# Keys and queries of a multi-mode delta rule: from normalised, turned windows to planes by feature with factors by token, and unread matmuls among the merges

## The chip, the cores and the metric

The kernel runs on one core of a Trainium2 chip. The metric is the device time of one launch in microseconds, the median of several runs. Engines are named as in the profile: PE (TensorE), DVE (VectorE), ACT (ScalarE), POOL (GpSimd) and SP (the queue that issues all transfers here).

## What is computed

The reference is a linear attention with a gated delta rule, followed by a mixture of experts, both with residuals. B=8 batches, T=512 tokens, D=128, H=8 heads, M=8 modes, DK=DV=64. All is 32-bit float.

```python
q, k, v = x@Wq, x@Wk, x@Wv                     # x is layer-normalised; (B,T,H,64)
beta, tg = sigmoid(x@Wbeta), sigmoid(x@Wtg)    # (B,T,H,M)
qr = _l2norm(_rotary(q, cos, sin)) * scale     # by mode: angles differ
kr = _l2norm(_rotary(k, cos, sin))
g = log(clip(tg * rho, 1e-6))
def step(S, inp):                              # over T, for each mode, batch, head
    S = S * exp(g)
    kv = einsum('mbhk,mbhkv->mbhv', k_t, S)
    S = S + k_t * ((v_t - kv) * beta)
    return S, einsum('mbhk,mbhkv->mbhv', q_t, S)
o = einsum('tmbhv,hm->bthv', ys, softmax(mode_logits)) * sigmoid(x@Wg)
x = x + o.reshape(B, T, H*DV) @ Wo             # then x + experts(layernorm(x))
```

A rotation does not change a vector's length, so the norm can be taken of q and k before it.

## The kernel before

`prepare` has two stages, and `recurrence` and `experts` follow, each behind a barrier of all engines (`fresh`).

**Projections** (`project`). A batch is 512 tokens in four tiles of 128. For each tile PE makes q, k, the gates z and v, with tokens as rows of the result (L285 to L294, 512 columns each but z). ACT copies q, k and v out of PSUM and squares q and k; DVE sums the squares by head (L418, L420). A batch later DVE multiplies keys and queries by one over their norm into `win` (L466), and POOL writes the first half of each once more with its sign turned (L504). `win` goes to memory as KQ_s, 192 floats for a token and head. `in_order` interleaves the tiles of batch b with the later work on batch b-1. ACT's chain at a batch's end is: square roots, exponentials, the copy of xT (L324), on which PE's next batch waits.

**Recurrence.** 64 sequences (head, batch), one in each step, `emit`. In step k the engines prepare sequence n+1 and run sequence n at the same time. Modes lie in 4 pairs, two halves of 64 partitions. Preparing: PE turns the window of keys and queries into features as rows (`transposes`, L1011, four groups of 8 matmuls) and ACT copies it to `kqT` (L793), one step ahead of its use; DVE rotates with the tables (`rotate`, L893, L894, L901), PE makes eight blocks of scores (L1053, L1057) and DVE multiplies them by decays (L926); DVE transposes them into lanes and solves 32x32 triangular systems there in 60 short instructions (`eliminate`), and two transposes bring the inverse back, TM (L954) and XO (L955). Running: PE merges the 32-blocks into 64-blocks at the head of the next step (`merge`: m=0 reads TM, L1034; m=1 reads XO and ZM, L1036; each in groups g=0, 1), then eight chunks in series, each through `read_state`, `solve_reads`, `keep_state` (L1108), `write_state`, with ACT moving R, W and S between them.

What sets the order on PE and ACT is a list of jobs (scores, merge(1,1), token_keys, turns) and a table, PE_PLACES and ACT_PLACES, which says how many jobs are taken at each of 16 places among the eight chunks. All matmuls run strictly in that order. One loop turn holds eight steps (one head); a barrier ends it. At k=6 SP also loads the next head's tables `tab`.

**Experts.** For each batch a `head` (gates, output projection, layer norm, routing) is cut into slots between the eight experts. In slots -1 and 0 DVE multiplies o by the gate (L1464), two products of 512 columns in each. PE makes both halves of an expert's hidden units (L1363, L1364) into banks that DVE's product with silu (L1527) must have left.

Of the kernel before, what the change touches and what calls it, by code (L numbers as in the profile page):

```python
# [24 lines left out]
HALF = DK // 2  # L25
# [51 lines left out]
def program(nc, x, Wq, Wk, Wv, Wbeta, Wtg, mode_logits, log_decay, omega_log, Wg, Wo, gate_w, w13, w2,  # L77
# [6 lines left out]
    KQ_s = dram("KQ_s", (H, B, 128, NT, 2 * WIN))  # L84
# [8 lines left out]
    with ExitStack() as whole:  # L93
# [7 lines left out]
        def fresh():  # L101
# [6 lines left out]
                c_mat, c_pos, c_col, ident, XN_s, KQ_s, V_s, G_s, EG_s, COL_s, TAB_s)  # L108
        recurrence(nc, sems, fresh, c_mat, ident, KQ_s, V_s, G_s, EG_s, COL_s, TAB_s, O_s)
        experts(nc, sems, fresh, x, Wg, Wo, gate_w, w13, w2, c_small, ident, XN_s, O_s, out)  # L110


def prepare(nc, sems, fresh, x, Wq, Wk, Wv, Wbeta, Wtg, mode_logits, log_decay, omega_log,
            c_mat, c_pos, c_col, ident, XN_s, KQ_s, V_s, G_s, EG_s, COL_s, TAB_s):
    with ExitStack() as ctx:
# [4 lines left out]
        wq, wk, wv = sb("wq", [128, H * DK]), sb("wk", [128, H * DK]), sb("wv", [128, H * DV])  # L120
        wbt = sb("wbt", [128, 2 * HM])
# [8 lines left out]
        with nc.Block() as block:  # L130
# [16 lines left out]
            def _(act):  # L147
# [4 lines left out]
                act.activation(modes[:, :, :], modes[:, :, :], ACT.Exp).then_inc(exp_out, 1)  # L152

            @block.vector
            def _(dve):
                v = Chain(dve, dve_s)
                dve.wait_ge(loaded, 11 * 16)
# [19 lines left out]
        project(nc, sems, fresh, x, wq, wk, wv, wbt, rho, tri, ones_c, ident, XN_s, raw, KQ_s, V_s, G_s, EG_s)  # L177
# [3 lines left out]
def project(nc, sems, fresh, x, wq, wk, wv, wbt, rho, tri, ones_c, ident, XN_s, raw, KQ_s, V_s, G_s, EG_s):  # L181

    with ExitStack() as ctx:
# [3 lines left out]
        def ps(name, shape):  # L187
# [7 lines left out]
        qk = sb("qk", [128, 2, 2, NT, H * DK])  # L195
        sqq = sb("sqq", [128, 2, 2, H * DK])
        ssq, less = sb("ssq", [128, 2, 2, NT, H]), sb("less", [128, 2, 2, NT, H])
        win = sb("win", [128, NT, H, 2 * WIN])
# [4 lines left out]
        QB, KB = [ps(f"q{i}", [128, 512]) for i in range(2)], [ps(f"k{i}", [128, 512]) for i in range(2)]  # L203
        VB, ZB = ps("v", [128, 512]), ps("z", [128, NT, 2 * HM])
        GB, TB = ps("g", [128, 2, NT, HM]), ps("t", [128, 512])

        (l_x0, l_x1, l_x2, dve_s, xn_done, xt_done, xt_copied, pe_q, pe_k, pe_z, pe_v, freed_q, k_copied, freed_k, freed_v,
         summed, std_in, std_out, ss_in, ss_out, logs_in, logs_out, decay_in, g_done, sums, gt_done, raw_s, exp_in, exp_out,
         lowered, flipped, q_done, halves, put_x0, put_x1, put_v0, put_v1, put_g, put_k) = sems[:39]
        l_x, put_x, put_v = (l_x0, l_x1, l_x2), (put_x0, put_x1), (put_v0, put_v1)  # L210

        def in_order(begin, tile, after, end):
# [1380 lines left out]
```

## Time and profile before

| | us |
|---|---|
| median of 3 runs | 4784.18 (4780.45 to 4792.02) |
| the profiled execution, its own time | 4793.02 |
| its span in the trace | 4790.8 |
| PE busy | 4015.4 (84%) |
| DVE busy | 3652.5 (76%) |
| ACT busy | 2902.2 (61%) |
| POOL busy | 371.3 (8%) |

A busy share says how long an engine had work, not that it set the time. The rows below give starts in microseconds from the span's start; "idle before" is how long the engine had stood before an instruction, with the instruction that released it. The granted clock of PE is given as a share of 2.4 GHz.

### The profile page before, as it was taken

The numbers are of one execution on the slowest core, as the hardware profiler recorded it, in microseconds if no ns is written. First come the engines' busy times: TensorE is split into PE (matmuls) and PEld (weight loads), VectorE is DVE, ScalarE is ACT, GpSimd is POOL, SyncE is SP. The second block draws the span as 40 slices with busy tenths as digits, with TensorE's granted clock in tenths as the row PEclk, the third lists the DMA queues.
The fourth block names the chain that finished last, engine by engine and source line by source line (L and its number), as shares of the span: only waits on it lengthen the run. The fifth ranks groups of instructions, "written<-read, shape, count | busy, mean of one in ns | idle before, by whom it ended". The sixth has DMA issues, their size and how long they took to land. (4 is left out here: it accounts for less than half of the span.)

```text
span 4790.8 us, 195228 instructions
## 1 busy us (share of the span) xinstructions
PE 4015.4 (84%) x85713; PEld 3307.7 (69%) x85713; DVE 3652.5 (76%) x7742; ACT 2902.2 (61%) x9736; POOL 371.3 (8%) x156
## 2 busy tenths in 40 slices
PE   5502999889988998889889988898899889987999
PEld 2201777777777777777777777777777777775666
DVE  6754888778877887788778877887788778854655
ACT  5742666666666666666666666666566666654443
POOL 1221000000000000000000000000000000000000
PEclk8755889889888998899889988998899889988999
DMA  4675222322232223222322231223122312203110
GB/s 119 167 182 133 52 51 56 83 53 52 52 87 53 52 52 87 53 52 52 87 53 52 52 87 47 57 52 87 40 59 58 82 44 58 57 10 83 36 31 7
DMA packets 283082, 314.77 MB, mean 66 GB/s; under 512 B 135768, under 2 KB 182752, under 8 KB 278112
## 3 DMA queue, kind: packets, MB, share of 16 engines
q1 hardware_dynamic: 282208, 301.99, 26.7%
q8 instruction: 687, 11.26, 1.0%
q14 instruction: 187, 1.53, 0.1%
HBM read 232.70 MB, written 69.21 MB: 63 GB/s over the span
## 5 line engine op out<-in xcount | busy, mean ns | idle before, releaser
L926 DVE TENSOR_TENSOR run_SC<-run_SP,run_DB 128x512 f32<-128x512 f32 x512 | 350.1, 687 | 474.6 <-PE run_SP L1057 468.3
L943 DVE TENSOR_TENSOR run_XL<-run_XL,run_EL 128x30 f32<-128x30 f32 (+14 forms) x1920 | 637.3, 332 | 66.0
L942 DVE TENSOR_TENSOR run_EL<-run_AL,run_XL 128x30 f32<-128x30 f32 (+14 forms) x1920 | 636.7, 332 | 66.0
L1053 PE MATMUL run_SP<-run_KP 64*32 64x128 f32 x8192 | 624.8, 302 | 24.5 <-DVE run_KP L901 12.7
L980 POOL TENSOR_TENSOR run_DB<-run_DB,run_below 128x2048 f32<-128x2048 f32 x64 | 297.9, 4655 | 3613.7 <-DVE run_XL L943 3487.9
L801 ACT ACTIVATE run_DB<-run_DB,run_col 128x64 f32<-128x64 f32 x2048 | 537.3, 337 | 12.0 <-POOL run_DB L980 4.2
L1053 PEld LDWEIGHTS run_SP<-run_KP 64*32 64x32 f32 x8192 | 465.6, 119 | 101.8 <-issue 50.0
L859 ACT COPY run_S<-run_KS 128x256 f32<-128x256 f32 x448 | 166.9, 373 | 556.5 <-PE run_KS L1118 556.5
L808 ACT ACTIVATE run_KD<-run_PR,run_col 128x64 f32<-128x64 f32 x2048 | 471.6, 327 | 12.9 <-PE run_PR L1073 6.8
L846 ACT ACTIVATE run_R<-run_KS,run_col 128x64 f32<-128x64 f32 x1792 | 416.0, 323 | 102.8 <-PE run_KS L1082 102.4
L1057 PE MATMUL run_SP<-run_KP 64*32 64x64 f32 x8192 | 454.5, 243 | 0.0
L1036 PE MATMUL run_PR<-run_XO,run_ZM 32*64 32x32 f32 x8192 | 422.9, 275 | 36.9 <-ACT run_ZM L778 36.6
L893 DVE TENSOR_TENSOR run_tmpv<-run_tab,run_kqT 128x512 f32<-128x512 f32 x512 | 372.2, 727 | 104.7 <-ACT run_kqT L793 37.6
L1011 PE MATMUL run_PR<-ident,run_win 128*64 128x128 f32 x4096 | 299.8, 283 | 178.0 <-DMA run_win<-KQ_s 154.0
L1036 PEld LDWEIGHTS run_PR<-run_XO,run_ZM 32*64 32x64 f32 x8192 | 406.1, 202 | 50.6 <-ACT run_ZM L778 41.5
L850 ACT ACTIVATE run_Sdec<-run_S,run_decay 128x64 f32<-128x64 f32 x1536 | 413.5, 364 | 0.0
L1094 PE MATMUL run_WP<-run_V,run_XN 64*64 64x64 f32 x8192 | 375.9, 237 | 39.9 <-issue 39.1
L1011 PEld LDWEIGHTS run_PR<-ident,run_win 128*64 128x64 f32 x4096 | 238.9, 141 | 208.7 <-DMA run_win<-KQ_s 154.3
L1073 PE MATMUL run_PR<-ident,run_KP 64*64 64x64 f32 x8192 | 294.1, 221 | 92.8 <-ACT run_KD L808 90.8
L1094 PEld LDWEIGHTS run_WP<-run_V,run_XN 64*64 64x64 f32 x8192 | 325.0, 152 | 65.9 <-issue 65.9
L1073 PEld LDWEIGHTS run_PR<-ident,run_KP 64*64 64x64 f32 x8192 | 260.8, 134 | 146.5 <-issue 142.2
L1125 PE MATMUL run_OB<-run_W,run_SC 128*64 128x64 f32 x4096 | 361.5, 234 | 0.5 <-ACT run_W L853 0.5
(201 smaller groups left out, 7588.8 us busy)
## 6 DMA issues: line engine op xcount, KB each, us to landing
run_DB<-G_s SPq DMA_DIRECT2D x256, 256.0 KB
run_EG<-EG_s SPq DMA_DIRECT2D x128, 512.0 KB, 8.9
run_tab<-TAB_s SPq DMA_DIRECT2D x128, 256.0 KB, 10.5
KQ_s<-proj_win SPq DMA_DIRECT2D x32, 768.0 KB, 7.8
run_win<-KQ_s SPq DMA_DIRECT2D x64, 384.0 KB, 3.1
TAB_s<-tab_tab SPq DMA_DIRECT2D x128, 128.0 KB, 2.4
run_V<-V_s SPq DMA_DIRECT2D x128, 128.0 KB, 2.6
V_s<-proj_vv SPq DMA_DIRECT2D x64, 128.0 KB, 3.1
```

Source lines behind the costliest of these rows:

```text
L801: last = act.activation(DB[:, p, c, :], DB[:, p, c, :], ACT.Exp, bias=col[:, par, 0, p, c:c + 1])
L808: last = act.activation(KD[:, par, p, c, :], token_rows[:, c % 2, p, :], ACT.Copy, scale=col[:, par, 2, p, c:c + 1])
L846: last = act.activation(R[:, p, :], KS[:, 0, p, :], ACT.Copy, scale=col[:, now, 1, p, c:c + 1])
L850: last = act.activation(Sdec[:, p, :], S[:, c % 2, p, :], ACT.Copy, scale=decay[:, now, p, c:c + 1])
L942: v.link(dve.tensor_tensor(e, bcast(AL[:, r + 1:, r], 2, done), bcast(XL[:, r, 0:done], 1, rows), ALU.mult))
L943: less = dve.tensor_tensor(XL[:, r + 1:, 0:done], XL[:, r + 1:, 0:done], e, ALU.subtract)
L1011: last = pe.matmul(PR[1][64 * e:64 * e + 64, 128 * i:128 * i + 128], win[:, i, off:off + DK], ident[:, :], start=True, stop=True)
L1036: last = pe.matmul(to[64 * e:64 * e + SPAN], ZM[two, p, c, :], XO[two, p, c, :], start=True, stop=True)
L1053: pe.matmul(out[64 * e:64 * e + C, p].rearrange("p (z u) i -> p z (u i)", z=2), KP[f, par, p, t0:t1], KP[f, kq, p, t0:t0 + SPAN], start=Tr ...
L1057: last = pe.matmul(out[64 * e + C:64 * e + SPAN, p, 0::3, :], KP[f, par, p, t1:t1 + C], KP[f, kq, p, t1:t1 + C], start=True, stop=True)
L1073: last = pe.matmul(token_rows[f, z, p, :], KP[f, par, p, t0:t0 + SPAN], ident[f, f], start=True, stop=True)
L1094: last = pe.matmul(WP[f, 0, p, :], XN[f, p, c, :], V[f, now, c, :], start=(p == 0), stop=(c == 0 and p == PAIRS - 1))
```

## The change

Keys and queries are no longer normalised and no longer turned. `project` computes them with features as rows: the weights are now the stationary operand and xT the moving one. A plane of the negated first halves comes from a third matmul with negated weights `wn`. The sums of squares are matmuls of the squares with `pair`, two columns of ones. Norms become factors by token: beta is divided by the squared key norm (added to the argument of its logarithm), v is multiplied by the key norm when DVE takes it out of PSUM, and one over the query norm goes to memory as RQ_s and is applied to o in `experts`. KQ_s has planes of 512 tokens for each feature, which six transfers put straight into `kqT` (`load_kq`). POOL has no work left in `project`.

In the recurrence the turns on PE and their copies on ACT are gone, the places are shifted accordingly, `token_keys` alternates between two banks, and `stay_busy`, a matmul whose result nothing reads, stands twice ahead of merge(0,0) (not in the first step of a loop turn), once behind it and once behind merge(0,1).

```diff
-    KQ_s = dram("KQ_s", (H, B, 128, NT, 2 * WIN))
+    KQ_s = dram("KQ_s", (H, B, 2, DK + HALF, T))
+    RQ_s = dram("RQ_s", (B, 128, NT, H))
...
+                for query, w in enumerate((wk, wq)):
+                    act.activation(wn[:, query], w[:, :].rearrange("p (h d) -> p h d", h=H)[:, :, 0:HALF], ACT.Copy, scale=-1.0).then_inc(exp_out, 1)
...
+                def square_sums(b, i):
...
+                    for query in range(2):
+                        pe.wait_ge(freed[query], n + 1)
+                        for t in range(NT):
+                            last = pe.matmul(SB[:, query, t, 2 * i:2 * i + 2], squares[:, n % 2, query, 128 * t:128 * t + 128], pair[:, :],
+                                             start=True, stop=True)
+                    last.then_inc(pe_ss, 1)
...
-                    pe.matmul(QB[n % 2][:, :], lhsT, wq[:, :], start=True, stop=True).then_inc(pe_q, 1)
-                    pe.matmul(KB[n % 2][:, :], lhsT, wk[:, :], start=True, stop=True).then_inc(pe_k, 1)
+                    for query, w in enumerate((wk, wq)):
+                        if n:
+                            pe.wait_ge(freed[query], n)
+                        pe.matmul(FB[query][:, :], w[:, 128 * i:128 * i + 128], xT[:, b % 2], start=True, stop=True).then_inc(pe_f[query], 1)
+                    if n:
+                        pe.wait_ge(freed_n, n)
+                    pe.matmul(NB[:, :], wn[:, i % 2, 4 * (i // 2):4 * (i // 2) + 4, :].rearrange("p h d -> p (h d)"), xT[:, b % 2],
+                              start=True, stop=True).then_inc(pe_n, 1)
...
+                def values(b, i):
+                    dve.wait_ge(pe_v, NT * b + i + 1)
+                    dve.tensor_tensor(vv[:, b % 2, i, :, :], VB[:, :, :], bcast(root[:, b % 2, 0, i, :], 2, DV), ALU.mult).then_inc(valued, 1)
...
-            @block.gpsimd
-            def _(pool):
-                def after(b, i):
...
+                    def load_kq(n):
+                        of = KQ_s.rearrange("h b z f t -> (h b) z f t")[bass.ds(n, 1)]
+                        for e in range(2):
+                            at = 64 * e
+                            for rows, planes, feats in ((slice(at, at + DK), 0, slice(0, DK)), (slice(at, at + HALF), 1, slice(HALF, DK)),
+                                                        (slice(at + HALF, at + DK), 1, slice(DK, DK + HALF))):
+                                sp.dma_start(kqT[rows, planes::2, :], of[:, :, feats].rearrange("a z f t -> f (a z) t")).then_inc(l_kq, 16)
...
                         if more:
                             n = n0 + (k + 2)
-                            sp.wait_ge(scored, SUPER * k + 2)
-                            if k + sets:
-                                sp.wait_ge(pe_t, 4 * (k + sets))
-                            load_win(n)
+                            sp.wait_ge(rot_k, NT * (k + 1))
+                            sp.wait_ge(rot_q, NT * (k + 1))
+                            load_kq(n)
                             sp.wait_ge(scored, SUPER * (k + 1))
                             load_g(n)
...
-                            turn = [(lambda r=r: transposed(k + sets, r)) if more else (lambda: None) for r in range(4)]
-                            jobs += ex + keys[0:4] + turn[0:2] + keys[4:6] + turn[2:3] + keys[6:8] + turn[3:4]
+                            jobs += ex + keys
...
-                                if k + sets:
-                                    dve.wait_ge(act_t, 4 * (k + sets))
+                                here(dve, l_kq, 6, k)
...
+                        def stay_busy():
+                            pe.matmul(KS[:, 0].rearrange("p a v -> p (a v)"), ident[:, :], Sdec[:, :, :].rearrange("p a v -> p (a v)"),
+                                      start=True, stop=True)
...
                         if runs:
+                            if k:
+                                stay_busy()
+                                stay_busy()
                             merge(0, 0)
+                            stay_busy()
                             merge(0, 1)
+                            stay_busy()
                             merge(1, 0)
...
+                            dve.wait_ge(l_r[b % 2], 16 * (b // 2 + 1))
+                            heads = o[:, b % 2, i, :].rearrange("p (h v) -> p h v", h=H)
+                            dve.tensor_tensor(heads, heads, bcast(rq[:, b % 2, i, :], 2, DV), ALU.mult).then_inc(scaled, 1)
+                            dve.wait_ge(scaled, NT * b + i + 1)
                             dve.tensor_tensor(o[:, b % 2, i, :], o[:, b % 2, i, :], gate[:, i, :], ALU.mult).then_inc(gated, 1)
```

The order of PE at the end of a step and the head of the next, before (from the second to the third step of a loop turn; OB are the outputs, PR the bank of merges and turns):

```order
L1011 MATMUL run_PR<-ident,run_win 64x128 x8
L1103 MATMUL run_WP<-run_R,run_XN 64x64 x8
L1073 MATMUL run_PR<-ident,run_KP 64x64 x16
L1125 MATMUL run_OB<-run_W,run_SC 64x64 x4
L1011 MATMUL run_PR<-ident,run_win 64x128 x8
L1034 MATMUL run_PR<-run_TM,run_SC 32x32 x64
L1036 MATMUL run_PR<-run_XO,run_ZM 64x32 x32
```

And the same place now:

```order
L1071 MATMUL run_WP<-run_R,run_XN 64x64 x8
L1098 MATMUL run_OB<-run_W,run_SC 64x64 x4
L1081 MATMUL run_KS<-run_Sdec,ident 128x256 x2
L1002 MATMUL run_PR<-run_TM,run_SC 32x32 x32
L1081 MATMUL run_KS<-run_Sdec,ident 128x256
L1002 MATMUL run_PR<-run_TM,run_SC 32x32 x32
L1081 MATMUL run_KS<-run_Sdec,ident 128x256
L1004 MATMUL run_PR<-run_XO,run_ZM 64x32 x32
```

Turns and the last token_keys have left the end of the step; three places of unread matmuls stand around the two first merges.

The order of PE in the projections, one tile of a batch in the steady part, before:

```order
L285 MATMUL proj_bank_q<-set_wq,proj_xT 128x512
L288 MATMUL proj_bank_k<-set_wk,proj_xT 128x512
L291 MATMUL proj_bank_z<-set_wbt,proj_xT 128x128
L294 MATMUL proj_bank_v<-set_wv,proj_xT 128x512
```

And now:

```order
L313 MATMUL proj_bank_f<-proj_xT,set_wk 128x512
L313 MATMUL proj_bank_f<-proj_xT,set_wq 128x512
L316 MATMUL proj_bank_n<-proj_xT,set_wn 128x512
L320 MATMUL proj_bank_z<-set_wbt,proj_xT 128x128
L301 MATMUL proj_bank_s<-set_pair,proj_squares 128x2 x8
L331 MATMUL proj_bank_v<-set_wv,proj_xT 128x512
```

A fourth matmul of 512 columns and eight of 2 columns have come into each tile.

## Rows read from the trace of the kernel before

**Rows 1.** Busy time by stage: us, then PE, PEld, DVE, ACT, POOL busy (x), PEclk, DMA share, GB/s
```profile
0.00:277.00 277.00, 135.22 (x384) 68.44 (x384) 170.00 (x311) 161.94 (x285) 50.21 (x69) 0.78 0.56 152
...
476.00:4250.00 3774.00, 3367.41 (x81532) 2883.08 (x81534) 3082.93 (x6381) 2425.20 (x8891) 285.69 (x63) 0.88 0.26 59
...
4314.00:4791.00 477.00, 432.80 (x2137) 288.47 (x2137) 268.40 (x831) 201.03 (x284) 0.00 (x0) 0.96 0.18 40
```

**Rows 2.** DVE transpose that ends a step: duration, first and last start
```profile
L955 DVE STREAM_TRANSPOSE run_XO<-run_XL x64: 1881/1936/1999, 476.3 to 4269.4; 128x1024 f32<-128x1024 f32 x64
```

**Rows 3.** DVE waits of the whole recurrence: us, times, longest us
```profile
DVE run_SC L926 <- PE run_SP L1057: 468.3, 300, 5.7
DVE run_tmpv L893 <- ACT run_kqT L793: 37.6, 7, 6.2
DVE run_tmpv L893 <- issue: 37.3, 6, 7.0
```

**Rows 4.** DVE timeline, two steps: start, us, instruction, [idle before <-releaser]
```profile
1991.12 1.94 DVE L955 STREAM_TRANSPOSE run_XO<-run_XL 128x1024 f32<-128x1024 f32 x1
...
2006.67 0.69 DVE L926 TENSOR_TENSOR run_SC<-run_SP,run_DB 128x512 f32<-128x512 f32 x1 [1.51 <-PE run_SP L1057]
...
2011.32 0.69 DVE L926 TENSOR_TENSOR run_SC<-run_SP,run_DB 128x512 f32<-128x512 f32 x1 [0.34 <-PE run_SP L1057]
...
2013.55 0.69 DVE L926 TENSOR_TENSOR run_SC<-run_SP,run_DB 128x512 f32<-128x512 f32 x1 [0.84 <-PE run_SP L1057]
...
2016.92 0.69 DVE L926 TENSOR_TENSOR run_SC<-run_SP,run_DB 128x512 f32<-128x512 f32 x1 [2.08 <-PE run_SP L1057]
...
2020.03 0.69 DVE L926 TENSOR_TENSOR run_SC<-run_SP,run_DB 128x512 f32<-128x512 f32 x1 [0.62 <-PE run_SP L1057]
2023.41 0.69 DVE L926 TENSOR_TENSOR run_SC<-run_SP,run_DB 128x512 f32<-128x512 f32 x1 [2.68 <-PE run_SP L1057]
...
2050.96 1.94 DVE L955 STREAM_TRANSPOSE run_XO<-run_XL 128x1024 f32<-128x1024 f32 x1
...
2073.16 0.69 DVE L926 TENSOR_TENSOR run_SC<-run_SP,run_DB 128x512 f32<-128x512 f32 x1 [1.47 <-PE run_SP L1057]
...
2076.27 0.69 DVE L926 TENSOR_TENSOR run_SC<-run_SP,run_DB 128x512 f32<-128x512 f32 x1 [0.62 <-PE run_SP L1057]
2079.64 0.69 DVE L926 TENSOR_TENSOR run_SC<-run_SP,run_DB 128x512 f32<-128x512 f32 x1 [2.68 <-PE run_SP L1057]
```

**Rows 5.** Two step starts by windows, columns as in rows 1
```profile
1993.00:2010.00 17.00, 16.21 (x304) 14.69 (x301) 15.46 (x26) 9.74 (x27) 0.78 (x1) 0.50 0.09 25
...
2054.00:2061.00 7.00, 6.48 (x114) 5.79 (x114) 7.00 (x13) 5.67 (x16) 0.00 (x0) 0.52 0.01 3
```

**Rows 6.** PE timeline of the later step, columns as in rows 4
```profile
2054.52 3.63 PE L1036 MATMUL run_PR<-run_XO,run_ZM 32*64 32x32 f32 x64 [1.20 <-ACT run_ZM L778]
...
2060.97 2.10 PE L1036 MATMUL run_PR<-run_XO,run_ZM 32*64 32x32 f32 x64
...
2068.01 0.70 PE L1108 MATMUL run_KS<-run_Sdec,ident 128*128 128x256 f32 x2
```

**Rows 7.** The last four us before a rotation that waited for kqT
```profile
2342.00:2346.00 4.00, 2.63 (x56) 2.35 (x56) 0.00 (x0) 2.54 (x12) 0.00 (x0) 1.00 0.09 23
```

**Rows 8.** PE timeline of the projections; all copies of xT, first and last start
```profile
131.74 2.07 PE L285 MATMUL proj_bank_q<-set_wq,proj_xT 128*128 128x512 f32 x2 [11.84 <-ACT proj_xT L324]
...
L324 ACT COPY proj_xT<-proj_bank_t x8: 567/567/586, 26.3 to 215.0; 128x512 f32<-128x512 f32 x8
```

**Rows 9.** PE timeline of the experts: small matmuls, then w13 matmuls
```profile
4471.54 0.96 PE L1341 MATMUL moe_ebank<-moe_gwT,moe_x2T 128*128 128x8 f32 x8
...
4492.40 1.02 PE L1363 MATMUL moe_ebank<-moe_x2T,moe_w13T 128*128 128x512 f32 x2
4493.26 1.02 PE L1364 MATMUL moe_ebank<-moe_x2T,moe_w13T 128*128 128x512 f32 x2
```

**Rows 10.** DVE timeline of the experts: hidden units after the gate
```profile
4490.56 1.28 DVE L1527 TENSOR_TENSOR moe_hid<-moe_sil,moe_ebank 128x512 f32<-128x512 f32 x2
```

More of the change, by code:

```diff
@@ L156, in _ @@
                 v = Chain(dve, dve_s)
+                v.link(dve.memset(pair[:, :], 0.0))
+                for h2 in range(2):
+                    v(dve.memset(pair[64 * h2:64 * h2 + 64, h2:h2 + 1], 1.0))
                 dve.wait_ge(loaded, 11 * 16)
@@ L296, in after, with end @@
+                def end(b):
+                    square_sums(b, NT - 1)
                 def after(b, i):
+                    if b or i:
+                        pe.wait_ge(valued, NT * b + i)
+                    pe.matmul(VB[:, :, :].rearrange("p h d -> p (h d)"), xT[:, b % 2, 128 * i:128 * i + 128], wv[:, :], start=True, stop=True).then_inc(pe_v, 1)
                     if i != 2:
@@ L309, in after @@
                     last.then_inc(sums, 1)
-                in_order(begin, tile, after, lambda b: None)
+                in_order(begin, quarter, after, end)
             @block.scalar
@@ L484, in after @@
                             dve.wait_ge(lowered, B)
[L486 to L508 removed]
+                in_order(begin, quarter, after, end)
         fresh()
@@ L807, in token_keys @@
                             for p in range(PAIRS):
-                                last = act.activation(KD[:, par, p, c, :], token_rows[:, c % 2, p, :], ACT.Copy,
+                                last = act.activation(KD[:, par, p, c, :], token_rows[c // 2 % 2][:, c % 2, p, :], ACT.Copy,
                                                       scale=col[:, par, 2, p, c:c + 1])
                             last.then_inc(kd_done, 1)
-                        if first and k == 0:
-                            for r in range(4):
-                                transposed(0, r)
                         if runs:
@@ L1149, in _ @@
                             kd = [lambda c=c: token_keys(c) for c in range(GROUP)]
-                            wins += more
-                            turned += more
-                            turn = [(lambda r=r: transposes(k + sets, r)) if more else (lambda: None) for r in range(4)]
-                            jobs = sc[0:1] + jobs + sc[1:] + kd[0:2] + turn[0:2] + kd[2:3] + turn[2:3] + kd[3:4] + turn[3:4]
+                            jobs = sc[0:1] + jobs + sc[1:] + kd
                         if not runs:
```

248 lines of the change are left out of this document (94 added, 154 removed).

## The prediction

> **What bounds the kernel now.** I read the stages first [rows 1]: the recurrence, from 476 to 4250 us, is 79% of the span. In it PE is busy 3367 of 3774 us and VectorE (DVE) 3083, so busy shares alone do not name the bound. The order of waiting does. One step (prepare sequence n+1, run sequence n) ends with the DVE transpose run_XO; between its first and its last start lie 63 steps in 3793.1 us, 60.2 us each [rows 2]. DVE's waits in the whole recurrence [rows 3] are 468.3 us for scores from PE (L926), 37.6 us for the turned keys kqT at 7 steps, and 37.3 us of "issue" at 6 of the loop's barriers. Per step that is 7.4 + 0.6 + 0.6 us, which leaves 51.5 us in which DVE works without pause: rotations, scores, elimination, transposes. DVE is therefore the ring that closes each step, and only its waits can be had.
>
> Two steps in a row show what the score waits are made of [rows 4]. From 1991.12 to 2050.96 (59.84 us) they are 1.51 + 0.34 + 0.84 + 2.08 + 0.62 + 2.68 = 8.07 us; in the next step 1.47 + 0.62 + 2.68 = 4.77. The last two, for scores 6 and 7, are the same to 0.01 us in both: they come from PE's place in the order late in the score phase and not from how the step began. What differs is the beginning. The granted clock stood at 0.50, which is 1.2 GHz, for 17 us after the first XO and for nearly 7 us after the second [rows 5]. A merge of 64 rows with ZM as one operand (L1036) takes 3.6 us then and 2.1 us at 2.4 GHz [rows 6]. PE was busy for 16.2 of the 17 us. What preceded both falls was a gap on PE and then the merges, which use 32-row tiles.
>
> **Part 1, the turning goes.** Out of each step go 4 groups of 8 matmuls (16 rows of L1011) and 4 copies to kqT on ScalarE (ACT). In ordinary steps they lie under DVE's elimination, and I take 0 for them. At the seventh step of each group of eight they are late: DVE waits 37.6 us / 7 = 5.4 us for kqT [rows 3], at a time when the DMA share has already fallen to 0.09 [rows 7], so the tables have landed and only the tail of PE and ACT is awaited. Without turns the rotation needs the outputs of PE and the tables. I leave 1 us: 7 x 4.4 = -31 us. Bounds: 0 (the tail is not shorter) and -38.
>
> **Part 2, kqT comes by DMA.** load_kq issues 6 transfers (128 x 4 x 512 floats, 1.05 MB) once all rotations are done, before load_g; in place of one of 128 x 4 x 192 floats, 0.39 MB, near the same point. SP's queue behind them holds load_g and load_eg, which wait for later signals in any case. Nothing needs kqT until the next step, some 35 us later. Price 0; if it starved PE, see rival D.
>
> **Part 3, the unread matmuls.** Each is 2 rows of 128x256, the form of keep_state, 0.63 us at 2.4 GHz by the 2 rows of 0.70 us with their overlap [rows 6]. The one before merge(1,0) and the one between the first merges fall into PE's 1.20 us wait for ZM [rows 6]: 2 x 0.63 = 1.26, so 0.1 us net. The two at the head of a step have no wait ahead of them and run in the gap after the last outputs. At 1.2 GHz they would cost twice that and 1.3 us would lie in the open. What they can give is the clock at 2.4 GHz through merges and first scores. Then the 1.5 us wait and the three others of a slow start go, and 0.62 + 2.68 = 3.3 us per step stays. Between 3.3 and today's mean of 7.4 I take 3.7, near the first, because the fall of the clock has followed the 32-row merges in both rows and full-array matmuls now stand among them; and 3 us more at 14 steps that begin after a barrier or after a table load. 63 x 3.7 + 14 x 3 = 275 us against 468.3: -193 us. Bounds: nothing regained, and 63 x 3.3 = 208, -260 us.
>
> The Trainium skill (TensorE: Matmul & The Clock Gate, HAM oscillation) says that a wait between groups of matmuls is enough to send the clock down again, each time. By it this change could lose: the tail is shorter, so the gap ahead of the first merge grows. That is rival A below. The rows of the two falls agree in that a gap came before both.
>
> **Part 4, the projections.** Per batch PE gets 16 matmuls of 512 columns for 12, and 8 groups of 4 matmuls with 2 moving columns, the sums of squares. A 512-column matmul is 0.86 us at 2.4 GHz (its 2 rows cover 1.02, and 0.86 lie between starts [rows 9]), so +3.4 us. The nearest row for the sums is L1341: 4 matmuls with 8 columns cover 0.96 us, less the same 0.15 of overlap 0.81 [rows 9]: 8 x 0.81 = 6.5 us. Today a batch takes 27.0 us (xT's first and last copy, 7 batches apart), and PE waits 11.84 us of one for xT [rows 8]. Adding 9.9 to the other 15.2 gives 25.1, and of the wait I take 4 us as not to be filled, since square roots, exponentials, two table loads and the copy of xT follow each other there on ACT. 29.1 against 27.0: +2.1 us x 8 = +17, and 1 for the tail. PE becomes the bound of this stage, ACT loses 4 copies and DVE 8 sums and 8 products, which I price at 0. Bounds: 0 (the gap takes it all) and +45, if half of the sums run at 1.2 GHz.
>
> The Trainium skill (TensorE: Matmul & The Clock Gate, Part 1) has starts of small matmuls no closer than about 25 ns; 64 rows at that floor would be 1.6 us a batch, and by it the stage would cost nothing more. The row says 101 ns, and I go by the row.
>
> **Part 5, small terms.** wn and its two ACT copies: +1. First step of all: DVE waits there for tables behind 0.66 MB more, at 152 GB/s [rows 1] +4. Experts: DVE scales o by rq, 32 products of 0.69 us, the form of L926, and 0.04 for each link. Four of them come before the hidden units of 4490.56 [rows 10], whose first half ends at 4491.2; PE's L1363 follows at 4492.40 [rows 9]. 4 x 0.73 = 2.9 us against 1.2 of slack: 1.7 us x 7 batches = +12. Bounds 0 and 20.
>
> **The sum** against the profiled execution: -31 - 193 + 18 + 1 + 4 + 12 = -189 us. That execution took 4793.0 us (span 4790.8), 8.8 above the median of 4784.2; so 4604 in its terms and **4595** in the median's. If everything open came out well (-38 - 260 + 5) it would be 4491; if only half of the clock's part came, 4691.
>
> **Rivals.**
> A, slower: the gap decides. With the turns gone PE ends earlier, the clock is down at the first merge of every step, and the four matmuls run at 1.2 GHz. All steps become like the first of [rows 4], 8.1 us of score waits, plus 1.3 us for the matmuls: 63 x (8.1 + 1.3) = 592 against 468, +124; with -31 and +35 that is +128, 4912. It takes the forecast's gain away from 3.0 us per step on (189 / 63). For it: PE's gaps precede the falls. Against it: full-array rows run at both sides of the gap. 0.06.
> B, no effect on the clock: waits stay at 7.4, hidden at 2.4 GHz: -31 + 35 = +4, 4788. 0.05.
> C, half held: -97 in place of -193, 4691. 0.09.
> D, the transfer: PE's stream is starved of instructions while 1 MB of kq moves in the score phase. Against it: the smaller load near this point leaves no stall in either step of [rows 4]. At the length of the third-last wait, 1.5 us, in each step: +94, 4689. 0.07.
> My forecast: 0.73, with its own range 4520 to 4650.
>
> **Chances and range.** The median moves by under 0.3% (14 us) without meaning, so that is my bound. Faster: forecast, C, D, 0.89, less 0.01 for mishaps with them: 0.88. Same: B, 0.05. Slower: A and what I did not see, 0.07. The range takes C and D in and A and B out: 4520 to 4715.
>
> **What would show it.** The clock over 476 to the end of the recurrence near 0.95 for 0.88. DVE's score waits near 275 us, with waits of 0.6 and 2.7 us still in each step and the 1.5 gone; no kqT row; steps near 55.2 us. PE without its 11.8 us wait in the projections and batches of 29 us. A wait of L1363 for hidden units of some 1.7 us more once a batch in the experts. The prediction is wrong if the clock is at 0.50 at most step starts, or if scores 6 and 7 wait longer than 3.3 us together because DVE, sooner there, meets the same PE.

## The result, and the profile after

The change made the kernel slower: 4917.3 us median (4910.8 to 4926.5) against 4782.3 (4780.5 to 4792.0), a ratio of 1.028, with a 95% interval of 1.026 to 1.030. The forecast was 4595, with a range of 4520 to 4715. The result is that of rival A, which was priced at 4912 and given a chance of 0.06.

The stages of the changed kernel by windows (columns as in [rows 1]), then the transpose that ends a step:

```profile
0.00:277.00 277.00, 215.04 (x942) 134.98 (x942) 116.06 (x240) 143.55 (x246) 0.20 (x4) 0.90 0.54 134
...
514.00:4365.00 3851.00, 3360.27 (x78344) 2802.30 (x78344) 3106.97 (x6427) 2294.21 (x8694) 285.01 (x63) 0.86 0.30 69
```

```profile
L945 DVE STREAM_TRANSPOSE run_XO<-run_XL x64: 1896/1932/1992, 513.9 to 4365.3; 128x1024 f32<-128x1024 f32 x64
```

Against [rows 2] this splits the difference of the two profiled executions (spans 4909.0 and 4790.8, 118 us) into three parts. Up to the first XO: 476.3 became 513.9, +37.6. The 63 steps between: 3793.1 became 3851.4, +58.3. After the last XO: 521.4 became 543.7, +22.3. The forecast had +23, -224 and +12 there, so it failed in the recurrence. The two ends together cost 59.9 us where 35 were priced.

Within the recurrence, 44 of the 58.3 us lie in the 48 steps that are neither the first nor the last of a loop turn (59.37 us for 58.46 in the mean). The eight first ones lost 28 (70.17 for 66.66), and the seven last ones gave 14 back (62.87 for 64.81).

DVE's waits in the changed recurrence, against [rows 3]:

```profile
DVE run_SC L916 <- PE run_SP L1025: 563.8, 301, 5.8
...
DVE run_tmpv L883 <- issue: 31.0, 6, 5.6
```

The row for kqT is gone, as forecast (-37.6). The score waits rose by 95.5 us where they were to fall by 193. The granted clock of the stage is 0.86, lower than the 0.88 of before. One step, among the slowest, shows how. These are PE's rows from the end of one step into the next (start, us, instruction, [idle before <-releaser]); the step's XO starts at 812.14:

```profile
807.03 0.68 PE L1098 MATMUL run_OB<-run_W,run_SC 128*64 128x64 f32 x8 [0.47 <-ACT run_W L844]
807.63 1.13 PE L1081 MATMUL run_KS<-run_Sdec,ident 128*128 128x256 f32 x4
812.30 1.92 PE L1002 MATMUL run_PR<-run_TM,run_SC 32*32 32x32 f32 x64 [3.54 <-DVE run_TM L944]
814.15 1.22 PE L1081 MATMUL run_KS<-run_Sdec,ident 128*128 128x256 f32 x2
815.30 1.92 PE L1002 MATMUL run_PR<-run_TM,run_SC 32*32 32x32 f32 x64
817.15 1.22 PE L1081 MATMUL run_KS<-run_Sdec,ident 128*128 128x256 f32 x2
818.30 3.62 PE L1004 MATMUL run_PR<-run_XO,run_ZM 32*64 32x32 f32 x64
821.85 0.42 PE L1021 MATMUL run_SP<-run_KP 64*32 64x128 f32 x2
```

The same place before the change, XO at 2050.96:

```profile
2048.38 1.04 PE L1011 MATMUL run_PR<-ident,run_win 128*64 128x128 f32 x14
2051.11 2.21 PE L1034 MATMUL run_PR<-run_TM,run_SC 32*32 32x32 f32 x128 [1.69 <-DVE run_TM L954]
...
2058.08 0.42 PE L1053 MATMUL run_SP<-run_KP 64*32 64x128 f32 x2
```

And the granted clock around that step of the changed kernel, by windows:

```profile
807.50:810.50 3.00, 1.27 (x8) 0.74 (x6) 2.66 (x11) 1.38 (x7) 0.25 (x1) 1.00 0.19 43
810.50:831.00 20.50, 18.70 (x356) 16.00 (x358) 16.36 (x23) 7.69 (x19) 4.30 (x1) 0.50 0.07 18
831.00:870.00 39.00, 34.70 (x882) 28.62 (x878) 31.17 (x74) 26.57 (x110) 0.00 (x0) 1.00 0.35 84
```

Before, the turns filled PE's tail and the wait for TM was 1.69 us. Now PE has only the outputs and the two leading unread matmuls there, then stands 3.54 us, and the clock is already at 1.2 GHz when the first merge starts. Both unread matmuls between the merges then take 1.22 us each (0.70 at 2.4 GHz, [rows 6]) in the path to the first scores. The first scores start 9.7 us after XO (821.85 - 812.14), where they started after 7.1 (2058.08 - 2050.96). DVE's waits in this step are on its own timeline:

```profile
830.30 0.69 DVE L916 TENSOR_TENSOR run_SC<-run_SP,run_DB 128x512 f32<-128x512 f32 x1 [4.11 <-PE run_SP L1025]
...
836.32 0.69 DVE L916 TENSOR_TENSOR run_SC<-run_SP,run_DB 128x512 f32<-128x512 f32 x1 [0.42 <-PE run_SP L1025]
...
839.70 0.69 DVE L916 TENSOR_TENSOR run_SC<-run_SP,run_DB 128x512 f32<-128x512 f32 x1 [2.09 <-PE run_SP L1025]
...
842.80 0.69 DVE L916 TENSOR_TENSOR run_SC<-run_SP,run_DB 128x512 f32<-128x512 f32 x1 [0.62 <-PE run_SP L1025]
```

With the last of 2.7 they are 9.9 us; before, the two steps of [rows 4] had 8.07 and 4.77.

Not every step is like this one. In 20 of the 48 ordinary steps the clock is at 1.2 GHz when the first merge starts: these take 60.9 us in the mean, with PE idle for 3.4 us ahead of the merge and the first scores 9.7 us after XO. In 23 it falls later, up to 2.8 us after XO: 58.6 us, 2.6 idle, scores after 8.6. The other five take 56.9. In the kernel before, none of the 48 had the clock down at the first merge, PE stood idle for 1.6 us in the mean (2.7 in the change), and the first scores came after 7.1. So what the ordinary steps lost lies in the 20. (These means are worked out from the trace, as in the table below.)

### The profile page after: what moved, and what is told of

Same layout as the page of the kernel before. It is cut to its first block and busy times, and to the rows that moved or that the text cites. A ratio compares the mean times of both kernels' runs of the same rounds, so it can differ in the third digit from the quotient of the medians.

```text
span 4909.0 us, 189436 instructions
## 1 busy us (share of the span) xinstructions
PE 4081.3 (83%) x82673; PEld 3281.1 (67%) x82673; DVE 3632.5 (74%) x7714; ACT 2740.6 (56%) x9450; POOL 321.1 (7%) x92
## 5 line engine op out<-in xcount | busy, mean ns | idle before, releaser
L916 DVE TENSOR_TENSOR run_SC<-run_SP,run_DB 128x512 f32<-128x512 f32 x512 | 352.2, 688 | 570.5 <-PE run_SP L1025 563.8
L1002 PE MATMUL run_PR<-run_TM,run_SC 32*32 32x32 f32 x8192 | 217.5, 222 | 261.4 <-DVE run_TM L944 132.5
L1004 PEld LDWEIGHTS run_PR<-run_XO,run_ZM 32*64 32x64 f32 x8192 | 393.2, 197 | 47.2 <-ACT run_ZM L782 24.1
L1002 PEld LDWEIGHTS run_PR<-run_TM,run_SC 32*32 32x32 f32 x8192 | 200.7, 137 | 320.4 <-issue 160.5
L1004 PE MATMUL run_PR<-run_XO,run_ZM 32*64 32x32 f32 x8192 | 409.8, 270 | 0.4 <-issue 0.4
L1071 PE MATMUL run_WP<-run_R,run_XN 64*64 64x64 f32 x7168 | 311.1, 227 | 118.2 <-ACT run_R L837 117.3
L1071 PEld LDWEIGHTS run_WP<-run_R,run_XN 64*64 64x64 f32 x7168 | 249.0, 136 | 191.6 <-ACT run_R L837 153.4
```

What stands on the lines that cost most here:

```text
L1002: last = pe.matmul(to[two], SC[one, 0, p, c, C:], TM[one, p, c, :], start=True, stop=True)
L1004: last = pe.matmul(to[64 * e:64 * e + SPAN], ZM[two, p, c, :], XO[two, p, c, :], start=True, stop=True)
L1071: last = pe.matmul(WP[f, 0, p, :], XN[f, p, c, :], R[f, p, :], start=False, stop=(p == PAIRS - 1))
```

## The experiments

Twelve kernels were run. Eleven differ in where unread matmuls (`stay_busy`) stand at the head of a step. `stay_busy` stands at up to six places: ahead of merge(0,0); between the groups of stage one (m=0); behind stage one; in the middle of merge(1,0); behind merge(1,0); in the middle of merge(1,1). The numbers in the table are how many stand at each. "Ordinary" is the mean step among the 48 that are neither first nor last of a loop turn. "Held" is how many of all 63 steps passed without the granted clock leaving 1.00. "Recurrence" is from the first XO to the last. These three are worked out from the starts of XO and the granted clock in each trace. The leading ones are left out in the first step of a loop turn everywhere; in the change, e2, e3 and e10 the two among the merges stand there too. Ratios are against the kernel before on the same chip.

| kernel | base | unread | median us | ratio (95%) | recurrence | ordinary | held |
|---|---|---|---|---|---|---|---|
| before | | none | 4782.3 | 1 | 3793.1 | 58.46 | 0 |
| the change | | 2,1,1,0,0,0 | 4917.3 | 1.028 (1.026 to 1.030) | 3851.4 | 59.37 | 1 |
| e1_no_unread | change | none | 4840.1 | 1.011 (1.008 to 1.015) | 3783.8 | 58.49 | 0 |
| e10_fill5 | change | 5,1,1,0,0,0 | 4909.7 | 1.028 (1.024 to 1.031) | 3843.2 | 59.42 | 5 |
| e3_fill9 | change | 9,1,1,0,0,0 | 4725.7 | 0.989 (0.986 to 0.992) | 3670.8 | 55.97 | 22 |
| e4_fill9_only | change | 9,0,0,0,0,0 | 4796.3 | 1.004 (1.003 to 1.006) | 3735.3 | 57.76 | 0 |
| e9_fill_hold1 | change | 9,1,0,1,0,0 | 4814.4 | 1.008 (1.004 to 1.011) | 3753.5 | 57.72 | 8 |
| e5_fill_hold | change | 9,1,1,1,1,1 | 4734.9 | 0.990 (0.985 to 0.994) | 3675.9 | 56.22 | 38 |
| e2_before_unread | before | 2,1,1,0,0,0 | 4707.2 | 0.982 (0.977 to 0.987) | 3706.9 | 56.74 | 24 |
| e8_before_hold1 | before | 3,1,0,1,0,0 | 4736.0 | 0.991 (0.988 to 0.994) | 3721.1 | 57.56 | 10 |
| e7_before_hold | before | 3,1,1,1,1,1 | 4680.7 | 0.978 (0.974 to 0.982) | 3676.7 | 56.09 | 41 |
| e12_before_six | before | 3,1,1,1,1,0 | 4622.5 | 0.966 (0.964 to 0.968) | 3626.1 | 55.26 | 40 |
| e11_small_tiles | before | 3,1,1,1,1,1 on 32x32 | 4937.2 | 1.033 (1.031 to 1.035) | 3926.1 | 60.74 | 0 |

**e1_no_unread.** All four taken out:

```diff
                         if runs:
-                            if k:
-                                stay_busy()
-                                stay_busy()
                             merge(0, 0)
-                            stay_busy()
                             merge(0, 1)
-                            stay_busy()
                             merge(1, 0)
```

> The changed kernel without its four unread matmuls. Theory G (the gap on PE between the last outputs and the first merge, 3.6 us where it was 1.5, lets the clock fall, and the unread matmuls among the merges, 1.2 us each at 1.2 GHz, then lie in the path): most steps still begin at 1.2 GHz, but the merges reach their second stage about 2 us sooner; 63 x 2 = 126 us less than the changed kernel, 4790 us, about the kernel before. Rival S (the unread matmuls do hold part of the clock, and without them it is worse): over 4920 us. Rival D (the keys' and queries' transfers starve PE): no change, 4917 us.

Measured 4840 us. The direction is theory G's, the size is not: 68 us came back in the recurrence, 1.1 per step for the 2 expected. So the four matmuls lost some 68 us net where they stand. The clock was down at the first merge in 45 of 48 ordinary steps here and in 20 with them, so they do hold something, and cost more than it is worth. The other 60 us of the loss are outside the recurrence.

**e2_before_unread.** The kernel before with the same four (and a memset of Sdec ahead of the loops):

```diff
                         if runs:
+                            if k:
+                                stay_busy()
+                                stay_busy()
                             merge(0, 0)
+                            stay_busy()
                             merge(0, 1)
+                            stay_busy()
                             merge(1, 0)
```

> The kernel before with the four unread matmuls alone added at the changed kernel's places. There the gap at a step's end is 1.5 us, and the two leading ones take 1.1 us of it. Theory G: the gap nearly closes, the clock stays at 2.4 GHz through the merges in most steps, and the waits of a slow start go; 60.2 us per step becomes 56 to 57, some 4570 us. Rival M (the 32-row merges bring the clock down whatever surrounds them, and the unread matmuls only cost): 4800 to 4900 us. In between, 4700 us, if the clock is held in half of the steps.

Measured 4707, the middle case (one of its four executions took 4661). The same four matmuls that cost 68 us in the changed kernel gain 86 in the recurrence of the kernel before. The clock was down at XO's start in no ordinary step, and 24 of 63 steps passed without a fall. The two kernels differ in all the rest of the change; what of it PE's rows show at this place is the end of the step, where the turns and the last token_keys still stand here (mean idle time ahead of the first merge 0.5 us, for 2.7).

**e3_fill9, e4_fill9_only, e10_fill5.** The changed kernel with the gap filled:

```diff
                             if k:
-                                stay_busy()
-                                stay_busy()
+                                for _ in range(9):
+                                    stay_busy()
                             merge(0, 0)
```

e4 also leaves out the one between the groups and the one behind them; e10 has five in place of nine.

> The changed kernel with nine leading unread matmuls in place of two, 0.56 us each at 2.4 GHz, so that PE has work from its last outputs to the first merge (3.6 us gap closed, 0.5 us over). Theory G: the clock stays at 2.4 GHz at most step starts outside barriers, steps take 54 to 55.5 us (the one step of the changed kernel whose clock never fell took 54.03), 48 x 5.5 = 264 us or more less: 4600 to 4650 us, granted clock of the recurrence over 0.93. Rival M (the merges bring it down themselves): 4917 us or more. Rival D: 4917 us or more.

> The same nine leading unread matmuls, and none between the merges. Theory G with the gap at the step's end alone as cause: as with the two between them or a little better, 4580 to 4640 us. If PE's short wait between the merges (1.2 us for ZM) is a second cause of the fall: the clock falls at 2 to 3 us into the step as in the kernel before, and it comes out near 4700 us.

> The changed kernel with five leading unread matmuls, the dose between two (4917 us) and nine (4726 us): 0.56 us each at 2.4 GHz, so the gap ahead of the first merge is 3.6 - 3 x 0.56 = 1.9 us. Theory G (the length of the gap decides): fewer steps begin at 1.2 GHz than with two, time between the two others, 4800 to 4850 us; if any gap under some 2 us is harmless, 4730 us. Rival (it is the number of full-array matmuls that counts and not the gap they close): also in between, but with the clock down at the first merge in as many steps as with two.

With nine, the changed kernel falls from 4917 to 4726, 1.1% under the kernel before. It also rules out rival D: its 22 steps without a fall take 54.1 us (median), 2.7 of them waits, with every kq transfer in place. It misses the 4600 to 4650 that G expected, and its rows show why. PE at the start of a step whose XO is at 2668.9:

```profile
2664.33 4.15 PE L1081 MATMUL run_KS<-run_Sdec,ident 128*128 128x256 f32 x18
2669.04 1.20 PE L1002 MATMUL run_PR<-run_TM,run_SC 32*32 32x32 f32 x64 [0.55 <-DVE run_TM L944]
2670.17 0.70 PE L1081 MATMUL run_KS<-run_Sdec,ident 128*128 128x256 f32 x2
2670.80 1.20 PE L1002 MATMUL run_PR<-run_TM,run_SC 32*32 32x32 f32 x64
2671.93 0.70 PE L1081 MATMUL run_KS<-run_Sdec,ident 128*128 128x256 f32 x2
2672.56 2.05 PE L1004 MATMUL run_PR<-run_XO,run_ZM 32*64 32x32 f32 x64
```

and the clock over it:

```profile
2668.90:2674.60 5.70, 5.56 (x196) 4.72 (x196) 5.67 (x8) 3.67 (x7) 2.62 (x1) 1.00 0.07 23
2674.60:2684.80 10.20, 9.63 (x170) 8.56 (x170) 9.48 (x16) 4.07 (x15) 0.00 (x0) 0.50 0.01 3
```

PE was busy for 5.56 of 5.70 us, and the clock fell all the same, behind the merges. In another step of this run, with XO at 1624.6, PE did not pause at all before the fall:

```profile
1621.60:1630.05 8.45, 8.45 (x206) 7.04 (x204) 8.24 (x12) 3.84 (x7) 4.57 (x1) 1.00 0.22 56
1630.20:1640.20 10.00, 9.74 (x172) 8.54 (x172) 9.28 (x16) 4.01 (x14) 0.00 (x0) 0.50 0.01 2
```

So the gap is not the only cause: falls also come at the end of the 32-row merges, with PE at work throughout. That it is the merges was still an argument here; e5 and e7 put it to the test. e4 and e10 say the same from two sides. Without the two among the first merges the fall comes in every step (none held); with the gap half closed the clock was up at XO's start in all 48 ordinary steps and down at the first merge in 5, but down 4 us after XO in 31, and nothing was gained. Theory G as I had put it, that the gap decides, fell here.

**e5_fill_hold and e7_before_hold.** Three more in stage two, and none in the first step of a loop turn:

```diff
+                                if m == 1 and k and p == 1:
+                                    stay_busy()
                             last.then_inc(pe_m, 1)
+                            if m == 1 and k and g == 0:
+                                stay_busy()
...
+                            if k:
+                                for _ in range(3):
+                                    stay_busy()
                             merge(0, 0)
+                            if k:
+                                stay_busy()
                             merge(0, 1)
+                            if k:
+                                stay_busy()
                             merge(1, 0)
```

(this is the kernel before; the changed one has nine ahead.)

> Nine leading unread matmuls as in the run before, one more in the middle of merge(1,0), one behind it and one in the middle of merge(1,1), in all steps but the first of a loop turn, where now none stands. Theory M2 (what is left of the falls, 5 to 6 us into half of the steps, comes from the 32-row merges of the second stage, which PE works at without a pause): the clock stays at 2.4 GHz through ordinary steps, which take 54 to 55 us for a mean of 56.0, and the first steps of a turn lose two unread matmuls of 1.2 us: 48 x 1.5 + 8 x 2.4 = 91 us less than with nine alone, 4635 us. Rival W (the falls follow short waits of PE in the first scores, so the added matmuls only cost their 0.6 us): 4710 to 4740 us.

> The kernel before, with its turning, norms and projections as they were, and unread matmuls alone: three ahead of merge(0,0) in place of two, one between the merges of the first stage, and one in the middle of merge(1,0), behind it and in the middle of merge(1,1), none in the first step of a loop turn. Theory M2: ordinary steps 54 to 55 us for the 56.7 of the run with four: 4707 - 48 x 2 - 10 = 4600 us. Rival W: 4700 to 4730 us. Against the fill in the changed kernel it shows what the rest of the change is worth once the clock is held: if turning costs nothing under DVE's elimination, this one is faster by the projections and experts, some 50 us less what the late kqT costs at 7 steps (30 us).

M2 was right on the cause: the falls 5 to 6 us into ordinary steps are gone (one is left, in e7), the clock stood at 2.4 GHz through 38 and 41 of 63 steps, and most of the others are the last two or the first of a loop turn. It was wrong on the time: 4735 and 4681. The first of these is what rival W had forecast (4710 to 4740), though its cause is not the one seen. The held steps have 4.6 and 4.2 us of waits (medians) where e3's have 2.7: two of the three new matmuls stand ahead of the first scores, which now come 7.6 and 7.5 us after XO for 6.5, and the third ahead of the second ones. The pair also prices the rest of the change at a held clock, if the nine leading matmuls of the one and the three of the other fill their gaps alike: recurrences of 3675.9 and 3676.7 us, so no gain from taking the turns out shows there. Of the 51 us between the two profiled executions, 40 lie up to the first XO and 13 behind the last.

**e8_before_hold1 and e9_fill_hold1.** Against e7 and e5, none behind stage one, and one in place of three in stage two:

```diff
-                                if m == 1 and k and p == 1:
+                                if m == 1 and k and g == 0 and p == 1:
                                     stay_busy()
-                            if m == 1 and k and g == 0:
-                                stay_busy()
...
                             merge(0, 1)
-                            if k:
-                                stay_busy()
                             merge(1, 0)
```

> The kernel before with three leading unread matmuls, one between the two groups of merge(0,.), and one in the middle of merge(1,0); none in the first step of a loop turn. In the run with seven the clock never fell in ordinary steps, but each step kept 0.8 to 2 us of score waits ahead of the last two, and 0.6 of the seventh. If one unread matmul in the second stage is enough to hold the clock, and the two taken away are 1.2 us of the path: ordinary steps near 54.5 us for 56.1, 4681 - 48 x 1.5 = 4610 us. If the clock falls again at 5 us into half of the steps: 4690 to 4700 us.

> The changed kernel with nine leading unread matmuls, one between the groups of the first stage, and one in the middle of merge(1,0); none in the first step of a loop turn. As for the kernel before: if the clock is held, 4735 - 48 x 1.5 = 4660 us; if it falls at 5 us in half of the steps, 4730 to 4750. Against the run beside it this one should be slower by the projections and the experts, 35 to 60 us, if turning on PE costs nothing once the clock is held.

Both lost: only 10 and 8 steps held, 4736 and 4814 us, each above the bad case of its expectation (4700 and 4750). In 33 and 39 of the 48 ordinary steps the clock fell within 8 us after XO. The two lie 78 us apart for the 35 to 60 expected; 32 of it are in the recurrence.

**e12_before_six.** This is e7 without the unread matmul in the middle of merge(1,1). (e7 has eight unread matmuls and this one seven; the expectations say seven and six.)

```diff
-                                if m == 1 and k and p == 1:
+                                if m == 1 and k and g == 0 and p == 1:
                                     stay_busy()
```

> The best run so far without the unread matmul in the middle of merge(1,1): six for seven. If the clock is held all the same, the first score wait of 0.8 us in ordinary steps becomes 0.2 or none: 4681 - 48 x 0.6 = 4652 us. If it falls at 6 us into a third of the steps: 16 x 2.5 = 40 us more, 4700 us.

Measured 4622.5 us, 3.4% under the kernel before and 6.0% under the change: the fastest here. PE from the end of a step on:

```profile
1976.67 1.56 PE L1118 MATMUL run_KS<-run_Sdec,ident 128*128 128x256 f32 x6
1978.23 1.20 PE L1035 MATMUL run_PR<-run_TM,run_SC 32*32 32x32 f32 x64
1979.36 0.70 PE L1118 MATMUL run_KS<-run_Sdec,ident 128*128 128x256 f32 x2
1979.98 1.20 PE L1035 MATMUL run_PR<-run_TM,run_SC 32*32 32x32 f32 x64
1981.12 0.70 PE L1118 MATMUL run_KS<-run_Sdec,ident 128*128 128x256 f32 x2
1981.74 1.12 PE L1037 MATMUL run_PR<-run_XO,run_ZM 32*64 32x32 f32 x32
1982.80 0.70 PE L1118 MATMUL run_KS<-run_Sdec,ident 128*128 128x256 f32 x2
1983.42 1.12 PE L1037 MATMUL run_PR<-run_XO,run_ZM 32*64 32x32 f32 x32
```

The window over five ordinary steps, and DVE's waits of the recurrence:

```profile
1923.20:2197.60 274.40, 259.50 (x6565) 215.81 (x6566) 246.04 (x512) 190.99 (x706) 22.89 (x6) 1.00 0.25 56
```

```profile
DVE run_SC L927 <- PE run_SP L1062: 308.1, 183, 5.8
DVE run_tmpv L894 <- ACT run_kqT L794: 40.6, 8, 6.8
```

Steps of 54.9 us (274.4 / 5), the clock at 1.00, score waits of 308 us for 468. That is what the forecast had hoped for from the change (275 us, 55.2 us a step), with the turns still in. The held steps have 3.4 us of waits (median) for e7's 4.2.

**e11_small_tiles.** e7 with each unread matmul on a 32x32 tile:

```diff
-                            pe.matmul(KS[:, 0].rearrange("p a v -> p (a v)"), ident[:, :], Sdec[:, :, :].rearrange("p a v -> p (a v)"),
+                            pe.matmul(KS[0:32, 0].rearrange("p a v -> p (a v)"), ident[0:32, 0:32], Sdec[0:32, :, :].rearrange("p a v -> p (a v)"),
                                       start=True, stop=True)
```

> The kernel before with the seven unread matmuls of the best run so far (three leading, one between the groups of stage one and one behind, three in stage two), each on a 32x32 tile of the array and 256 columns in place of 128x128 and 256, so that PE is as long at work on them but with a sixteenth of the array. If what holds the clock is that PE has no pause, it is held as with the large ones: 4680 us, clock near 0.93. If it is how much of the array is at work: the clock falls at 1.7 to 5 us into most steps as in the kernel before, and the matmuls then cost 1.2 us each: 4860 to 4950 us, clock under 0.87.

Measured 4937 us. PE at a step's start, XO at 2092.0:

```profile
2090.82 1.48 PE L1118 MATMUL run_KS<-run_Sdec,ident 32*32 32x256 f32 x6
...
2093.13 0.40 PE L1118 MATMUL run_KS<-run_Sdec,ident 32*32 32x256 f32 x1
2093.16 0.38 PE L1035 MATMUL run_PR<-run_TM,run_SC 32*32 32x32 f32 x14
...
2095.55 1.27 PE L1037 MATMUL run_PR<-run_XO,run_ZM 32*64 32x32 f32 x32 [0.73 <-ACT run_ZM L779]
```

and the clock from 4.5 us behind XO on:

```profile
2096.50:2113.50 17.00, 17.00 (x251) 13.05 (x250) 12.83 (x22) 7.26 (x26) 0.00 (x0) 0.50 0.08 25
```

The three leading ones take 1.48 us, as the large ones do (1.56), and no step was held, against 41 with the large ones. Full-array matmuls hold the clock, these do not. The run is not quite the test it was meant to be: among the merges the small ones run beside them (2093.13 and 2093.16), so that a pause of 0.73 us ahead of stage two stays. That a fall needs no pause is shown by e3's step at 1624.6. A comparison with small matmuls that leave no pause was not run.

**e6_terms_out.** The changed kernel with two computations left out, for the terms outside the recurrence:

```diff
-                        for t in range(NT):
+                        for t in range(1):
                             last = pe.matmul(SB[:, query, t, 2 * i:2 * i + 2], squares[:, n % 2, query, 128 * t:128 * t + 128], pair[:, :],
...
-                    dve.tensor_scalar(ssq[:, b % 2], SB[:, :, :, :], 1e-6, None, ALU.add).then_inc(ss_in, 1)
+                    dve.tensor_scalar(ssq[:, b % 2], bcast(SB[:, :, 0, :], 2, NT), 1e-6, None, ALU.add).then_inc(ss_in, 1)
...
-                            dve.tensor_tensor(heads, heads, bcast(rq[:, b % 2, i, :], 2, DV), ALU.mult).then_inc(scaled, 1)
-                            dve.wait_ge(scaled, NT * b + i + 1)
```

> The changed kernel with two computations left out: three quarters of the square sums on PE in the projections (norms are taken of one tile in four), and the scaling of the attention output by one over the query norm in the experts. If the square sums on PE set the batch (31.0 us for 27.0 before), the last batch's copy of xT comes at some 216 us for 243.8, and the stage of the tables starts 28 us sooner; if the wait for ACT's chain or the transfers of the planes set it, it stays within 5 us. If DVE's scaling is what the experts lost, their 22 us come back. Both: 4867 us; neither: 4917 us.

Measured 4893 us. The copies of xT, here and in the change:

```profile
L358 ACT COPY proj_xT<-proj_bank_t x8: 567/567/587, 26.3 to 226.6; 128x512 f32<-128x512 f32 x8
```

```profile
L358 ACT COPY proj_xT<-proj_bank_t x8: 567/567/585, 26.5 to 243.8; 128x512 f32<-128x512 f32 x8
```

A batch took 27.0 us before [rows 8], 31.0 in the change and 28.6 here. Three quarters of the square sums are worth 17 us of the stage (243.8 to 226.6), not the 28 expected. From the last XO to the end it is 523.5 us for 543.7, so the scaling of o is nearly all of the 22 us that the experts lost. The recurrence, whose code is untouched, took 3877.9 us for 3851.4. Recurrences of one trace each can thus differ by 26 us without a cause in the code, and smaller differences in the table's column prove nothing.

## Why the prediction was wrong

**The frame was right.** DVE's waits set the step, and at a held clock 3.3 us of them stay: 32 of e12's 48 ordinary steps have score waits of 3.3 to 3.5 us, and five steps in a row took 54.9 us each. (Of the 51.5 us that the prediction calls work without pause, 48.9 are DVE's busy time, 3083 / 63; the rest are smaller waits.)

**Part 3 failed, in its last inference.** It said that the clock would hold "because the fall of the clock has followed the 32-row merges in both rows and full-array matmuls now stand among them". The runs show two things that bring the fall, a gap (two leading matmuls against nine) and a run of 32-row merges (e3 against e5), and the four matmuls answer neither in full. I counted the two leading ones as work in the gap and did not subtract what the removed turns had done there: the wait for TM went from 1.69 to 3.54 us in the steps shown. Part 1 had priced the same removal at a gain. The estimate of -193 became +95.5 in score waits. The matmuls were also priced at 0.1 us net among the merges, at 2.4 GHz; at 1.2 GHz they are 1.22 each, and the net cost of all four was some 68 us (e1).

**Rival A** had the direction and nearly the sum: 9.4 us per step of waits and matmuls against a measured 563.8 / 63 = 8.9, and 4912 us against 4917. Partly this is luck. It had +93 us in the recurrence (124 - 31) for the measured 58, and 35 outside for 60. Its condition, the clock down at the first merge of every step, was met in 20 of 48 ordinary steps. It was held for unlikely because full-array rows stand at both sides of the gap. That speaks of the edges, while between them PE stood idle for 3.4 us in those 20.

The Trainium skill (TensorE: Matmul & The Clock Gate, HAM oscillation) has waits between groups of matmuls as the cause of repeated falls. The change's trace agrees with it in the step shown (3.54 us ahead of a merge at 0.50). e3's trace shows falls that it does not cover: there the clock fell with PE busy for 8.45 of 8.45 us.

**Part 1**, -31: the kqT waits did go (-37.6), but with the turns gone and nothing put in (e1) the recurrence was only 9 us shorter, less than two traces can tell apart; the score waits took the rest (497.4 for 468.3). At a held clock no gain showed (e5, e7).

**Part 2**, 0: right. e3's held steps, with six transfers each, take 54.1 us.

**Part 4**, +18: the stage after the projections started 32.6 us later, 28.6 of it in seven batch distances (31.04 us in the mean for 26.96) and 4 behind them. Two batches of the change by windows, and PE's waits in the stage:

```profile
83.92:117.60 33.68, 29.23 (x120) 17.91 (x120) 14.61 (x29) 18.20 (x32) 0.00 (x0) 0.85 0.63 154
117.60:148.35 30.75, 26.07 (x120) 16.71 (x120) 14.61 (x29) 18.10 (x32) 0.00 (x0) 0.94 0.70 169
```

```profile
PE proj_bank_f L313 <- ACT proj_xT L358: 27.7, 8, 4.1
...
PE proj_bank_v L331 <- DVE proj_vv L472: 11.0, 8, 7.5
```

A batch with the clock at 0.94 takes 30.7 us: 26.1 of PE's work (25.1 forecast; the square sums take 59.0 / 8 = 7.4 for the 6.5 priced), 4.1 for xT (4 forecast) and 0.5 for v. The same places before were 28.9 apart, so this is +1.8, near the forecast's +2.1. The forecast took the wait of one such batch (11.84) from the mean of seven (27.0), which a first batch of 18.5 us had lowered: its 29.1 should have been 30.9. What it missed is elsewhere. In three of the seven batches the granted clock was 0.81 to 0.85, PE was busy for 29.0 to 29.4 us, and they took 33.3 to 34.0; the bound of +45 had this case. The first batch had only 5.0 us of wait to fill and went from 18.5 to 24.1. In the last batch, behind its copy of xT, PE waits 7.5 us at once for DVE to take v out of its bank, which is now a product that itself waits for the norms, an edit that was priced at 0; that this made the 4 us behind the seven distances is not shown.

**Part 5**: the first XO came another 5 us later than the stage before it explains, for the +4 of the first step. Experts +22 for +12. PE's waits there:

```profile
PE moe_ebank L1337 <- DVE moe_hid L1505: 12.8, 8, 1.7
PE moe_ebank L1298 <- DVE moe_o L1442: 11.9, 7, 1.9
```

The wait for hidden units, which I expected to grow, was 12.7 us before and is 12.8. The new one stands at the transposes of o (L1298), 1.7 us in each of seven batches: size and count as forecast, at another instruction. Another 8 us went with the scaling in e6, but where they lie was not shown. The stretch behind the last XO took 536.7 to 544.3 us in the kernels with the change's experts and 521.4 to 525.0 in those with the old ones, so two traces give anything from 12 to 23 us.

## What to carry over

Before work is taken off a busy engine, look at what it fills: on PE the turns were free under DVE's work, and the pause that they left behind was not: without them and without unread matmuls (e1) the score waits rose by 29 us, which ate most of what the missing kqT waits gave. Unread matmuls were worth their place here only where enough stood in every gap and every run of small tiles to hold the clock throughout; two fewer than the best (e8 against e12) gave 0.991 for 0.966, one more (e7) 0.978. Try such fillers on the old kernel alone first: here that was faster (0.982, at best 0.966) than the change they came with.

## What was not expected of the hardware

In e3 the clock fell to 1.2 GHz behind 4.45 us of 32-row merges (1.20 + 1.20 + 2.05) with 1.4 us of full-array matmuls among them and no gap over 0.6 us, and in another step behind the same merges with no gap at all. It stayed down for 10 us in which PE was busy 9.63 and 9.74. Eight matmuls of 128x256 on the full array held it in 41 steps (e7), eight of 256 columns on a 32x32 tile in none (e11). The dose at a step's end is steep: two and five leading ones gave the same time (1.028 both), nine took 4% off.
